# A perceiver block on one core: the first key tile in quarters, key passes around the transposes, and the first scores and values in rounds by pass

## The reference, cut to what matters

```python
def _L0_xattn_ref(q, k, v, Wq, bq, Wk, bk, Wv, bv):
    scale = jnp.asarray(np.sqrt(QK_DIM), q.dtype)          # QK_DIM = 128
    qp = jnp.einsum('bsd,ed->bse', q, Wq) + bq
    kp = jnp.einsum('bsd,ed->bse', k, Wk) + bk
    vp = jnp.einsum('bsd,ed->bse', v, Wv) + bv
    z = jnp.einsum('bqe,bke->bqk', qp, kp)
    z = jax.nn.sigmoid(z / scale)
    return jnp.einsum('bqk,bkd->bqd', z, vp)
...
x = x + _L0_xattn_ref(_layernorm(x, axis=-1), ctx_1024, ctx_1024, Wq, bq, Wk, bk, Wv, bv)
x = x + _L0_attn_ref(_layernorm(x, axis=-1), ...)
x = x + _L0_ffn_ref(_layernorm(x, axis=-1), ...)
```

## Time and profile before

| | us |
|---|---|
| three runs | 584.59, 585.00, 585.08 |
| median | 585.0 |
| the profiled execution | 584.42 |
| its span, first to last instruction | 582.6 |
| TensorE busy | 571.4 (98%) |
| VectorE busy | 448.5 (77%) |
| ScalarE busy | 392.8 (67%) |
| steady stream of one block (24 + 12 + 12 products) | 9.62 |

### The profile page before, as it was taken

The page is one execution under the profiler, slowest core; times in us unless marked ns, Lnnn a source line. Parts: engine busy times, 40 slices in busy tenths (PEclk is TensorE's granted clock), DMA queues, the critical chain, the costliest instruction groups (busy, mean ns, idle before and its releaser), DMA issues.

```text
span 582.6 us, 7921 instructions
## 1 busy us (share of the span) xinstructions
PE 571.4 (98%) x2966; PEld 472.8 (81%) x2966; DVE 448.5 (77%) x499; ACT 392.8 (67%) x529; POOL 1.7 (0%) x7
## 2 busy tenths in 40 slices
PE   7899999999999999999999999999999999999998
PEld 4788888888888888888888888888888885766787
DVE  5887878787878798889788978787878775786642
ACT  5776677776767787868786767777776772586321
POOL 1000000000000000000000000000000000000000
DMA  8678877777777877787778676767676752000200
GB/s 278 206 242 271 257 245 243 221 224 224 228 229 243 260 246 233 244 258 251 240 237 259 216 228 208 231 210 228 208 244 193 246 174 118 1 2 2 72 1 36
DMA packets 33094, 115.87 MB, mean 199 GB/s; under 512 B 4065, under 2 KB 4769, under 8 KB 32673
## 3 DMA queue, kind: packets, MB, share of 16 engines
q1 hardware_dynamic: 32480, 114.79, 62.4%
q10 hardware_dynamic: 576, 0.59, 0.3%
HBM read 114.84 MB, written 0.52 MB: 198 GB/s over the span
## 4 chain that ended last, share of the span: by engine, by line
PE 93%; DVE 3%; ACT 2%; DMA 1%; issue 1%; DVEq 0%; SPq 0%
PE ps L327 45%; PE ps L275 22%; PE ps L292 12%; PE ps L767 4%; PE ps L799 2%; PE ps L486 2%; PE ps L660 1%; PE ps L430 1%; ACT w L601 1%; DMA rawt<-in_ctxt 1%; PE ps L579 1%; DMA x_s<-in_x 1%; PE ps L608 1%; DVE zl L307 0%; DVE tl L204 0%
## 5 line engine op out<-in xcount | busy, mean ns | idle before, releaser
L327 PE MATMUL ps<-nh,zl 128*128 128x512 f32 x392 | 144.8, 390 | 0.4 <-DVE zl L307 0.3
L327 PE MATMUL ps<-nh,zh 128*128 128x512 f32 x392 | 144.9, 390 | 0.0
L327 PE MATMUL ps<-nl,zh 128*128 128x512 f32 x392 | 144.4, 389 | 0.0
L307 DVE TENSOR_TENSOR zl<-zf,zh 128x1024 fp32r<-128x1024 f32 x49 | 60.1, 1226 | 83.4 <-ACT zh L306 83.4
L216 DVE TENSOR_TENSOR nl<-rawn,nh 128x1024 fp32r<-128x1024 f32 x98 | 116.7, 1221 | 4.2 <-ACT nh L213 2.5
L204 DVE TENSOR_TENSOR tl<-rawt,th 128x1024 fp32r<-128x1024 f32 x98 | 115.6, 1218 | 2.2 <-ACT th L199 2.1
L213 ACT ACTIVATE nh<-rawn 128x1024 fp32r<-128x1024 f32 x98 | 101.6, 1056 | 14.1 <-DMA rawn<-in_ctxn 13.5
L199 ACT ACTIVATE th<-rawt 128x1024 fp32r<-128x1024 f32 x98 | 98.6, 1053 | 5.4 <-DMA rawt<-in_ctxt 5.4
L302 ACT ACTIVATE zf<-ps 128x512 f32<-128x512 f32 x98 | 58.2, 597 | 56.7 <-PE ps L292 51.1
L327 PEld LDWEIGHTS ps<-nh,zl 128*128 128x128 f32 x392 | 73.4, 188 | 17.0 <-DVE zl L307 1.7
L327 PEld LDWEIGHTS ps<-nh,zh 128*128 128x128 f32 x392 | 73.4, 188 | 15.6 <-issue 0.2
(11 more groups left out here) (154 smaller groups left out, 575.0 us busy)
## 6 DMA issues: line engine op xcount, KB each, us to landing
rawt<-in_ctxt SPq DMA_DIRECT2D x98, 512.0 KB, 4.7
rawn<-in_ctxn SPq DMA_DIRECT2D x98, 512.0 KB, 6.4
wst<-in_wg SPq DMA_DIRECT2D x4, 512.0 KB, 7.3
wst<-in_wu SPq DMA_DIRECT2D x4, 512.0 KB, 7.4
wds<-in_wd SPq DMA_DIRECT2D x4, 512.0 KB, 4.8
wv_s<-in_wvt SPq DMA_DIRECT2D x1, 1024.0 KB, 9.9
wq_s<-in_wq SPq DMA_DIRECT2D x1, 1024.0 KB, 7.1
wo_s<-in_wo SPq DMA_DIRECT2D x1, 1024.0 KB, 4.7
```

What stands on the lines that cost most here:

```text
L307: ZL[b] = put("vector", lambda e: e.tensor_tensor(zl[b % 2][:], zf[:], zh[b % 2][:], ALU.subtract), [ZH[b]] + av, "zl")
L327: AV[b] = put("tensor", lambda e, z=z, n=n, i=i, j=j, r=r: e.matmul(bank(4 + r), z[:, j * T + r * P:j * T + r * P + P], n[:, j * D:(j + 1) ...
```

## The change

- The query weights are loaded by SyncE, behind the first key tile.
- Key tile 0 comes in four loads of 512 columns (`dq0` to `dq3`), and both parts are made per quarter (`first_high`, `first_low`).
- ScalarE: the high part of quarter 0 stands ahead of the square root, those of quarters 1 to 3 behind it.
- VectorE: `h_s` twice, `wkl`, `hT`, then the four low quarters, then the query's low part, the keys' low part, the low parts of key tile 1, and only then that of value tile 0's first half. The second half of value tile 0 is split behind the weights of block 0, its high part too.
- TensorE: high products of quarters 0 to 2, four transposes, high product of quarter 3, four transposes, the four products with the weights' low part, the query projection, the four products with the tile's low part.
- Scores of block 0 run pass by pass over the four parts of keys, each pass waiting for its own operands. The accumulation is opened once for a bank (`start` with the first product of a bank) in all blocks.
- Values of block 0 run their first two parts of rows in rounds: high by high, high weights by low values, low weights by high values, four products each.
- The loads of value tile 1's first half stand on SyncE's list behind those of key tile 2.

```diff
--- before.py
+++ after.py
@@ -174,7 +174,6 @@
         DID = dma("scalar", id_s[:], ident, "did")
         wq0 = zf
         DBK = dma("scalar", bqk_s[:], bqk, "dbk")
-        DWQ = dma("scalar", wq0[:, 0:512], wqt, "dwq")
         ctn = ctxn.rearrange("(b p j) d -> b p (j d)", p=P, j=4)
 
         HALF = (slice(0, TILE // 2), slice(TILE // 2, TILE))
@@ -186,8 +185,9 @@
         def load_n(b, k):
             n_ld[b, k] = dma("sync", rawn[:, HALF[k]], ctn[b][:, HALF[k]], f"dn{k}", n_rd.get((b - 1, k), ()))
 
-        for k in range(2):
-            load_t(0, k)
+        QRT = [slice(512 * c, 512 * c + 512) for c in range(4)]
+        DT0 = [dma("sync", rawt[:, QRT[c]], ctxt[0][:, QRT[c]], f"dq{c}") for c in range(4)]
+        DWQ = dma("sync", wq0[:, 0:512], wqt, "dwq")
         for k in range(2):
             load_n(0, k)
 
@@ -230,6 +230,13 @@
         WARM = [put("scalar", lambda e: e.activation(sq[0:1, 1:2], sq[0:1, 0:1], ACT.Sqrt), [SQ0], "lnw")]
         WKH = put("scalar", lambda e: e.activation(wkh[:], wk_s[:], ACT.Copy), [DWK], "wkh")
 
+        TH0, TL0 = [], []
+
+        def first_high(c):
+            n = QRT[c]
+            TH0.append(put("scalar", lambda e: e.activation(th[:, n], rawt[:, n], ACT.Copy), [DT0[c]], "th"))
+            Th[0, c // 2] = TH0[c]
+
         def stat(k, n=2):
             return st[:, k:k + n]
 
@@ -239,29 +246,55 @@
             m = put("vector", lambda e, r=r: e.bn_stats(st[:, 6 * r:6 * r + 6], x_s[:, r, :]), [DX[r]], "ln")
             m = put("vector", lambda e, r=r: e.bn_aggr(mv[:, r, :], st[:, 6 * r:6 * r + 6]), [m], "ln")
         m = put("vector", lambda e: e.tensor_scalar(stat(16), mv[:, :, 1], EPS, None, ALU.add), [m], "ln")
+        first_high(0)
         m = put("scalar", lambda e: e.activation(stat(18), stat(16), ACT.Sqrt), [m], "lnq")
         m = put("vector", lambda e: e.reciprocal(stat(20), stat(18)), [m], "ln")
         m = put("vector", lambda e: e.tensor_tensor(stat(22), stat(16), stat(20), ALU.mult), [m], "ln")
         m = put("vector", lambda e: e.tensor_tensor(stat(24), stat(22), stat(18), ALU.add), [m], "ln")
         m = put("vector", lambda e: e.reciprocal(stat(26), stat(24)), [m], "ln")
-        hm = []
-        for r in range(2):
-            h = put("vector", lambda e, r=r: e.tensor_scalar(h_s[:, r, :], x_s[:, r, :], mv[:, r, 0:1], stat(26 + r, 1),
-                                                             ALU.subtract, ALU.mult), [m], "lnh")
+        def first_low(c):
+            n = QRT[c]
+            TL0.append(put("vector", lambda e: e.tensor_tensor(tl[:, n], rawt[:, n], th[:, n], ALU.subtract),
+                           [DT0[c], TH0[c]], "tl"))
+            Tl[0, c // 2] = TL0[c]
+            if c % 2:
+                t_rd[0, c // 2] = [TH0[c], TL0[c]]
+                load_t(1, c // 2)
+
+        def first_keys(w, t, c, wait, opens=False, closes=False):
+            return put("tensor", lambda e: e.matmul(bank(0), w[:, c * P:(c + 1) * P], t[:, QRT[c]], start=opens, stop=closes),
+                       wait, "kp" if closes else None)
+
+        def first_rows(r):
+            h = put("vector", lambda e: e.tensor_scalar(h_s[:, r, :], x_s[:, r, :], mv[:, r, 0:1], stat(26 + r, 1),
+                                                        ALU.subtract, ALU.mult), [m], "lnh")
             for k in range(4):
-                f = put("tensor", lambda e, r=r, k=k: e.transpose(bank(6 + r)[:, k * P:(k + 1) * P],
-                                                                  h_s[:, r, k * P:(k + 1) * P], id_s[:]),
+                f = put("tensor", lambda e, k=k: e.transpose(bank(6 + r)[:, k * P:(k + 1) * P],
+                                                             h_s[:, r, k * P:(k + 1) * P], id_s[:]),
                         [h, DID], "lnt" if k == 3 else None)
-            hm.append(f)
+            return f
+
+        for c in range(1, 4):
+            first_high(c)
+        for c in range(3):
+            first_keys(wkh, th, c, [WKH, TH0[c]], opens=c == 0)
+        hm = [first_rows(0)]
+        first_keys(wkh, th, 3, [TH0[3]])
+        hm.append(first_rows(1))
+        tp = [bank(6 + r).rearrange("p (c n) -> p c n", c=4) for r in range(2)]
         WK = put("vector", lambda e: e.tensor_tensor(wkl[:], wk_s[:], wkh[:], ALU.subtract), [WKH], "wkl")
-        low_a = split_t(0, 0)
-        low_a()
-        low_b = split_t(0, 1)
-        tp = [bank(6 + r).rearrange("p (c n) -> p c n", c=4) for r in range(2)]
         hm = [put("scalar", lambda e: e.activation(hT[:, :, 0:P], tp[0], ACT.Copy, scale=2.0), [hm[0]], "lne_a"),
               put("vector", lambda e: e.tensor_scalar(hT[:, :, P:T], tp[1], 2.0, None, ALU.mult), [hm[1]], "lne_v")]
         put("scalar", lambda e: e.activation(sq[0:1, 6:7], sq[0:1, 0:1], ACT.Sigmoid), [SQ0], "sgw")
-        low_b()
+        for c in range(4):
+            first_low(c)
+        for c in range(4):
+            first_keys(wkl, th, c, [WK])
+        for c in range(4):
+            QP_PE = put("tensor", lambda e, c=c: e.matmul(bank(6)[:, 0:T], wq0[:, c * P:(c + 1) * P], hT[:, c, :],
+                                                          start=(c == 0), stop=(c == 3)), hm + [DWQ], "qp" if c == 3 else None)
+        for c in range(4):
+            KP[0] = first_keys(wkh, tl, c, [TL0[c]], closes=c == 3)
 
 
         def keys(b, steps=range(3)):
@@ -284,15 +317,16 @@
                 op0=ALU.add, op1=ALU.subtract), [KPH[b]], "kpl")
 
         def scores(b):
-            for j in range(4):
+            turns = [(j, i) for j in range(4) for i in range(3)] if b else [(j, i) for i in range(3) for j in range(4)]
+            for j, i in turns:
                 o = bank(2 + j // 2)[:, T * (j % 2):T * (j % 2) + T]
                 js = slice(j * P, (j + 1) * P)
-                wait = [KPH[b], KPL[b], QP] + [ZF[k] for k in (b - 1,) if k in ZF]
-                for i, (k, w) in enumerate([(kph, qph), (kph, qpl), (kpl, qph)]):
-                    m = put("tensor", lambda e, o=o, js=js, k=k, w=w, i=i: e.matmul(
-                        o, k[:, js], w[:], start=(i == 0), stop=(i == 2)), wait,
-                        "s" if (i == 2 and j % 2) else None)
-                if j % 2:
+                k, w = [(kph, qph), (kph, qpl), (kpl, qph)][i]
+                wait = [[KPH[b], QPH], [QP], [KPL[b]]][i] + [ZF[k] for k in (b - 1,) if k in ZF]
+                m = put("tensor", lambda e, o=o, js=js, k=k, w=w, i=i, j=j: e.matmul(
+                    o, k[:, js], w[:], start=(i == 0 and j % 2 == 0), stop=(i == 2 and j % 2 == 1)), wait,
+                    "s" if (i == 2 and j % 2) else None)
+                if (i, j % 2) == (2, 1):
                     S[b, j // 2] = m
             S[b] = m
 
@@ -312,13 +346,16 @@
 
         def values(b, js=range(4), rs=(0, 1), sig="av"):
             n_h, n_l = nh[b % 2], nl[b % 2]
+            two = [(j, r) for j in (0, 1) for r in rs]
             passes = [(zh[b % 2], n_h), (zl[b % 2], n_h), (zh[b % 2], n_l)]
-            if len(rs) == 1 and js[0] == 0:
+            if b == 0:
+                turns = [(j, r, i) for i in (0, 2, 1) for j, r in two] + [(j, r, i) for j in (2, 3) for r in rs for i in range(3)]
+            elif len(rs) == 1 and js[0] == 0:
                 turns = [(j, rs[0], i) for i in (0, 2, 1) for j in js[:2]] + [(j, rs[0], i) for j in js[2:] for i in range(3)]
             else:
                 turns = []
                 for j in js:
-                    turns += [(j, r, i) for i in ((0, 2, 1) if b else (0, 1, 2)) for r in rs] if j == 0 else \
+                    turns += [(j, r, i) for i in (0, 2, 1) for r in rs] if j == 0 else \
                         [(j, r, i) for r in rs for i in range(3)]
             for j, r, i in turns:
                 z, n = passes[i]
@@ -330,21 +367,16 @@
                     wait, sig if (j, r, i) == (3, rs[-1], 2) else None)
             return AV[b]
 
-        keys(0)
-        for c in range(4):
-            m = put("tensor", lambda e, c=c: e.matmul(bank(6)[:, 0:T], wq0[:, c * P:(c + 1) * P], hT[:, c, :],
-                                                      start=(c == 0), stop=(c == 3)), hm + [DWQ], "qp" if c == 3 else None)
-        QP_PE = m
-        split_n(0, 0)
-        key_parts(0)
-        low_n = split_n(0, 1, later=True)
+        split_n0 = split_n(0, 0, later=True)
         QPH = put("scalar", lambda e: e.activation(qph[:], bank(6)[:, 0:T], ACT.Identity, bias=bqk_s[:, 0:1]),
                   [QP_PE, DBK], "qph")
         QP = put("vector", lambda e: e.scalar_tensor_tensor(
             out=qpl[:], in0=bank(6)[:, 0:T], scalar=bqk_s[:, 0:1], in1=qph[:], op0=ALU.add, op1=ALU.subtract),
             [QPH], "qpl")
+        key_parts(0)
         for k in range(2):
             split_t(1, k)()
+        split_n0()
 
         late = [(wv_s[:], wvt), (kvd_s[:], kvd), (qr_s[:], qrope), (kr_s[:], krope), (kup_s[:], kup),
```

(2 more changed lines are left out.)

## The result

The changed kernel takes 588.88 us (median of six runs, 587.57 to 589.61) against 584.56 (six runs, 584.45 to 585.08): ratio 1.0071, 95% interval 1.0059 to 1.0084. The direction was forecast, the size was not: 4.3 us slower where the sum gave 1.7, and outside the range. The profiled execution took 587.57 us for a span of 585.8, 3.15 us more than the one before.

The account below looks back on a forecast made before the run. TensorE's last early wait, behind two load chains, was taken to bound the kernel: profiled 584.4 plus 1.7 for the later second chain gave 586.1, and the timed median's 0.6 above the profiled run gave 586.7 us; range 584.7 to 588.2.

Parts of the forecast that it names:

- What bounds the kernel: Beginning: TensorE's last early wait, set by two chains, each through one load (key tile 1, value tile 1) and ScalarE's queue.
- TensorE after s: Block 0 values lose their 0.6 us wait; scores of block 1 start at s + 8.96 = 26.86, 0.5 us later.
- s: Start of ScalarE's copy of key tile 1's second half: 17.9, between 16.7 and 18.4, against 16.76 before.
- Second chain: Value tile 1's load goes out at s + 5.87 = 23.8; block 1's fifth value product at 33.4, 1.7 us later.
- Loads and high parts: Key tile 0 lands 0.65 us sooner, about 8.55, quarters costing nothing; VectorE can evict the second transposes at 9.95.
- Low parts: Four low quarters on VectorE behind the eviction take 2.5 us, end at 13.06, 1.13 us later; freed load out at 13.13.
- Scores of block 0: Start of TensorE's stream: scores done by 15.7, a gain of one to two microseconds that lands in a wait.
- L: Duration of the load of value tile 1's second half: 5.2 us taken, 4.8 before, range 4.8 to 6.1.
- rival C: Slow clock: TensorE, nearly idle from 13.4 to 17.9, falls to the 1.2 GHz level; 587.3 us; chance 0.05.
- A: Rival: no measurable change, both chain loads near their short ends; 585.0 to 586.1 us; chance 0.33.
- B: Rival: faster, s well below 16.76, fifth value product of block 1 1.3 us early; 583.7 us; chance 0.08.
- D: Rival: first quarter lands at 7, square root with it; everything from LayerNorm on 0.4 to 0.6 later, 587.2; chance 0.09.

Follow-up runs that it names:

- e3: Changed kernel with the low parts of quarters 0 and 1 ahead of VectorE's eviction of the transposes; 587.65 us, ratio 1.0064.
- e6: Changed kernel with low parts of quarters 0 and 1 ahead of VectorE's eviction, plus 17 products on zeros in TensorE's waits; 586.26 us, ratio 1.0022.
- e4: Changed kernel with 17 more products on zeros into an unused bank where TensorE waits; 587.49 us, ratio 1.0047.
- e1: The changed kernel run again, unchanged; 588.58 us, ratio 1.0069 to the kernel before.
- e2: Changed kernel with the bias load taken from ScalarE's list and issued by SyncE behind the value tile's loads; 588.58 us, ratio 1.0075.
- e7: Kernel before with only the change's rounds for scores and values of block 0; 585.11 us, ratio 1.0003.
- e8: Changed kernel with the split of value tile 1's second half moved behind the weights of block 1; 588.02 us, ratio 1.0053.
- e9: Kernel before with query weights behind key tile 0, low halves ahead of the eviction, block 0 rounds, late split of value tile 1's second half; 584.05 us, 0.9981.
- e12: Changed kernel with half loads, two low quarters before the eviction, 17 products on zeros, late split of value tile 1's second half; 585.52 us, 1.0009.

## Why the prediction was wrong in size

- **What bounds the kernel**: right. Both chains of the earlier trace rows are the chains of the changed kernel.
- **TensorE after s**: right to the hundredth. Scores of block 1 start at 27.70, which is 18.74 + 8.96. **Second chain**: right. The load goes out at 24.61 = s + 5.87, and from its landing to the low weights it is again 4.42 us.
- **Loads and high parts**: here the sum failed. "At about 8.55" for the whole tile holds for half loads (8.3 to 8.5); for quarters it was 9.7. I took the 400 GB/s of the earlier trace rows, measured while x and the key weights were loaded, for the quarters, and gave nothing for them: they moved 281 to 330. The third quarter, which I had near 7.9, was copied at 9.05 and gated the transposes; eviction at 11.38 instead of 9.95. Size of the error 1.4 us: 1.1 is the landing (the fourth quarter's copy started at 9.70 instead of 8.58), and 0.3 is TensorE's own list, where the third quarter's product and four transposes stood ahead of the fourth's product until 10.67. The 0.5 us that I worked out from the rate in the Trainium skill (DMA: Bandwidth & Descriptors, Bandwidth), which I set aside, pointed the right way; the landing here was 1.1 us late, with a spread of more than a microsecond between profiles.
- **Low parts**: right as a step (2.50 us for the four behind the eviction), as e3's rows show too; its time shows in e6 against e4.
- **Scores of block 0**: wrong by 1.7 us, without a price. I had them done by 15.7, one to two microseconds ahead of the kernel before; they came at 17.4, no sooner than there, since the last low quarter was late.
- **s**: 18.74 instead of 17.9, outside my 16.7 to 18.4. The load took 4.17 instead of 4.73, which gave 0.6 of the 1.4 back. **L**: 5.47 instead of 5.2. Together 2.87 instead of 1.7 by the fifth product.
- **The clock**: rival C was priced at +0.6 on the likeliest case and given 0.05. A mean clock of 0.997 was read in five of six runs of the changed kernel, in three of five of e1. I looked only at the idle time from 13.4 to 17.9; that before the third quarter, where I had expected products, counts as well: the one fall that a profile caught, in e2, is there and not behind 13.4. I used the 1.72 us idle before 8.06 as evidence that such gaps are harmless, from one execution. By runs of the changed kernel and e1, those at 1.000 (three) average 587.8 and those at 0.997 (eight) 588.9. The rule of the Trainium skill (TensorE: Matmul & The Clock Gate, Part 1), that idle time takes the clock back to half, agrees with e2's rows (0.54 from 9.65 to 13.07, behind a stretch with two products); the changed kernel's own profile, with as thin a stretch, stayed at 1.00. It deserved more than 0.05.
- **A, B, D**: A needed a value load of 4.8 us and B a last low part before 12.2; they were 5.47 and 14.49. D, the square root later, cost nothing by itself: 7.11 instead of 6.43, but the transposes waited for the third quarter, not for the rows, which were ready at 9.1.
- **The total**: 588.88 is 2.2 us above 586.7. Of these, 1.1 are the two chains up to the fifth value product, 0.3 come behind 480 us, where the sum had nothing, and 0.7 the distance of the median from the profiled run, 1.3 instead of 0.6, which by e4 is mostly the clock.

## What to carry to other kernels

Ask of every step that is split finer or moved earlier which load its last piece frees, and follow that load to the strictly ordered list in which others stand behind it: here the rounds saved TensorE 0.6 us in block 0 that were worth nothing (e7), while the low parts that free the next load went behind an eviction, which was worth a microsecond (e6 against e4). Put work that waits for a load behind the work that has its operands (e8, by its profile), and fill an engine's wait with what is ready (e3). When a change thins TensorE's work out in the beginning, reckon with the clock in part of the runs, and look at the clock of all runs, not only of the profiled one.

## What the runs showed of the hardware that I had not expected

- With key tile 0 in four 256 KB loads (2 KB rows out of rows of 8 KB), 140 to 354 GB/s were moved from 5 to 6 us; with two of 512 KB, 332 to 418; while x and the key weights were loaded, with rows of 2 KB that follow each other in memory, 400. Whether it is the row's length or its place in memory wasn't tried.
- The same load, in the same place, took 4.0 to 5.0 us in the profiles, and third quarters landed between 8.0 and 10.0 us: one profile of before is a weak base for a term that is a load's landing.
- In some executions of several kernels TensorE waits once more near the end of the stream (0.9 us in e6, 1.0 in e9, 1.4 in e12, none so long in the kernel before). It may add to the spread of the runs; its cause wasn't looked for.
